# Routed experts' second product with weights at rest and tokens in motion, for four of eight experts

## The reference, cut to what matters

```python
def _L1_ffn_ref(x, Wr, W1, b1, W2, b2, sW1, sb1, sW2, sb2):
    logits = xf @ Wr.T
    topv, idx = jax.lax.top_k(logits, K)                 # K = 2
    gate_k = jax.nn.softmax(topv, axis=-1)
    ...
    h = jax.nn.relu(jnp.einsum('td,ehd->teh', xf, W1) + b1)
    y = jnp.einsum('teh,edh->ted', h, W2) + b2
    moe = jnp.einsum('te,ted->td', gates, y)
    sh = jax.nn.relu(xf @ sW1.T + sb1) @ sW2.T + sb2
    return moe + 0.1 * K * sh
```

## Time and profile before

| | value |
|---|---|
| timed runs, median (lowest to highest) | 2266.35 us (2262.14 to 2268.36) |
| profiled execution, its own time | 2264.78 us |
| span of its profile | 2263.6 us |
| TensorE busy in the span | 87% |
| VectorE busy | 60% |
| ScalarE busy | 40% |
| routed experts, from H(0) of e = 0 to the end of Y(7) of e = 7 | about 1522 to 2235 us of the span |

### The profile page before, as it was taken

How to read it: one execution, slowest core, us unless ns; L and a number is a source line. 1 busy time by engine, 2 the same in 40 slices (tenths; PEclk the granted TensorE clock), 3 DMA queues, 4 the chain that set the end, 5 groups by cost and what they waited for, 6 DMA issues and landing times.

```text
span 2263.6 us, 30780 instructions
## 1 busy us (share of the span) xinstructions
PE 1961.5 (87%) x12259; PEld 1831.3 (81%) x12260; DVE 1361.4 (60%) x2445; ACT 895.7 (40%) x1433; POOL 212.0 (9%) x177
## 2 busy tenths in 40 slices
PE   5787989878997975688758999999999999999984
PEld 5675779878887975587647989999999989888883
DVE  5878666442335466688865475446565665666675
ACT  2212212313231421366633322325555555555662
POOL 0000000003000000565720000000000000000001
PEclk9998998996999987799979899999999999999997
DMA  8100002100111100200021112224655566566775
GB/s 324 42 24 20 22 22 91 49 3 27 56 64 58 66 31 29 72 20 34 15 98 66 45 61 96 79 96 178 214 185 212 200 226 219 204 226 223 264 285 186
DMA packets 40346, 250.73 MB, mean 111 GB/s; under 512 B 5436, under 2 KB 6838, under 8 KB 18184
## 3 DMA queue, kind: packets, MB, share of 16 engines
q1 hardware_dynamic: 32024, 219.33, 27.2%
q10 hardware_dynamic: 5424, 16.52, 1.8%
q0 software_dynamic: 2752, 12.88, 1.7%
HBM read 225.80 MB, written 22.91 MB: 110 GB/s over the span
## 4 chain that ended last, share of the span: by engine, by line
PE 67%; DVE 17%; issue 9%; ACT 4%; DMA 3%; POOL 1%; DVEq 0%; POOLq 0%; SPq 0%; ACTq 0%
PE bank L280 18%; PE bank L282 17%; PE bank L281 17%; PE bank L2340 6%; DVE weight_lo L254 3%; PE bank L533 3%; PE bank L2341 3%; ACT weight_hi L244 2%; DMA weight_raw<-in_ffn_w 1%; PE bank L2344 1%; DVE mix_kv_lo L301 1%; DVE mix_kv L1531 1%; DMA token_rows<-expert_rows,slot_row 1%; DVE weight_lo L301 1%; DVE xT_lo L301 1%
## 5 line engine op out<-in xcount | busy, mean ns | idle before, releaser
L254 DVE TENSOR_TENSOR weight_lo<-weight_raw,weight_hi 128x2304 fp32r<-128x2304 f32 (+1 forms) x180 | 453.0, 2523 | 233.6 <-ACT weight_hi L244 233.4
L244 ACT ACTIVATE weight_hi<-weight_raw 128x2304 fp32r<-128x2304 f32 (+1 forms) x180 | 375.5, 2093 | 168.8 <-DMA weight_raw<-in_ffn_w 138.5
L280 PE MATMUL bank<-weight_hi,hidden_hi 128*128 128x384 f32 (+4 forms) x912 | 310.4, 340 | 12.5 <-DVE weight_lo L254 10.6
L282 PE MATMUL bank<-weight_hi,hidden_lo 128*128 128x384 f32 (+4 forms) x912 | 308.5, 338 | 0.0
L281 PE MATMUL bank<-weight_lo,hidden_hi 128*128 128x384 f32 (+4 forms) x912 | 308.1, 338 | 0.0
L280 PE MATMUL bank<-xT_hi,weight_hi 128*128 128x306 f32 (+1 forms) x576 | 185.0, 321 | 6.3 <-DVE mix_kv L1533 2.5
L281 PE MATMUL bank<-xT_lo,weight_hi 128*128 128x306 f32 (+1 forms) x576 | 179.6, 312 | 0.0
L282 PE MATMUL bank<-xT_hi,weight_lo 128*128 128x306 f32 (+1 forms) x576 | 179.1, 311 | 0.0
L280 PEld LDWEIGHTS bank<-weight_hi,hidden_hi 128*128 128x128 f32 (+4 forms) x912 | 159.0, 174 | 24.7 <-DVE weight_lo L254 12.6
L280 PE MATMUL bank<-weight_hi,xT_hi 128*128 128x384 f32 (+1 forms) x480 | 162.3, 338 | 10.0 <-DVE xT_lo L301 4.5
L533 PE MATMUL bank<-one_hot_dst,one_hot_src 125*128 125x313 f16 x800 | 130.0, 316 | 45.6 <-DVE one_hot_dst L511 42.4
(11 more groups left out here) (401 smaller groups left out, 4303.7 us busy)
## 6 DMA issues: line engine op xcount, KB each, us to landing
weight_raw<-in_ffn_w SPq DMA_DIRECT2D x136, 1152.0 KB, 5.2
weight_raw<-in_shared_w SPq DMA_DIRECT2D x16, 1152.0 KB, 5.2
expert_rows<-bias_row ACTq DMA_DIRECT2D x1, 12288.0 KB, 39.4
weight_raw<-in_mix_kv SPq DMA_DIRECT2D x8, 1152.0 KB, 6.8
weight_raw<-in_gat_w SPq DMA_DIRECT2D x8, 768.0 KB, 4.3
weight_raw<-in_mix_q SPq DMA_DIRECT2D x4, 1152.0 KB, 5.2
weight_raw<-in_mix_out SPq DMA_DIRECT2D x4, 1152.0 KB, 5.1
weight_raw<-in_gnn_w SPq DMA_DIRECT2D x4, 1152.0 KB, 5.1
```

The source lines that it names most:

```text
L244: act.activation(whi[:, r, 0:width[i]], raw[:, r, 0:width[i]], ACT.Copy).then_inc(*w_hi.one())
L254: dve.tensor_tensor(wlo[:, r, 0:width[i]], raw[:, r, 0:width[i]], whi[:, r, 0:width[i]].bitcast(F32), ALU.subtract).then_inc(*w_lo.one())
L280: pe.matmul(dst, a[0], b[0], start=first, stop=False)
L282: return pe.matmul(dst, a[1], b[0], start=False, stop=last)
```

## The change

For experts e = 2 to 5 (`ASIDE`; widths 208, 176, 160, 160) the second product is turned round. `w2` is at rest, 128 of its 768 output columns at a time, and the hidden units of all tokens move, upper and lower side by side. The sums come out transposed, one bank for each of six groups d of output columns, so they take six banks (2 to 7) and leave the ring two (0 and 1) for as long as these experts last. During the next expert's chunks 0 and 1 ScalarE copies the upper columns of each bank to `yT`, VectorE adds the lower columns (`y_out`). In its chunks 1 to 4 TensorE transposes `yT` back, one piece of three transposes a chunk behind Y, and ScalarE copies the piece to `yt`. The copy at the expert's end goes away for these four. For all experts the gathered tokens are turned one piece a chunk (chunks 1 to 4) in place of all in chunk 1. On ScalarE and VectorE the piece comes ahead of the chunk's two weight tiles.

```diff
+ASIDE = range(2, 6)
-        hT = tuple(part[:, :, :, 0:CAP] for part in hs)
+        hp = [part... "p (m a n) -> p m a n", m=3, a=2) for part in hs]
-        slot_bank, y_banks = psum[7], psum[4:8]
+        slot_bank, y_banks, yT_banks = psum[7], psum[4:8], psum[2:8]
+        Y_OUT = {(0, 0): (0, 1), (0, 1): (2, 3), (0, 2): (4,), (1, 0): (5,)}
+        def pieces(e, c):
+            return [c - 1] if e < E and 1 <= c <= 2 * len(tiles_of[e]) else []
...
+            def aside(bank, w, d, h, width, first, last):
+                both, one = bank[:, 0:2 * width].rearrange("p (a n) -> p a n", a=2), bank[:, 0:width]
+                hi, lo = at(w, ALL, ALL, slice(d * P, (d + 1) * P))
+                for k in range(3):
+                    if k < 2:
+                        pe.matmul(both, hi[:, k, :], h[:, k, :, 0:width], start=(first and k == 0), stop=False)
+                        pe.matmul(one, lo[:, k, :], h[:, k, 0, 0:width], start=False, stop=False)
+                    else:
+                        pe.matmul(one, lo[:, k, :], h[:, k, 0, 0:width], start=False, stop=False)
+                        end = pe.matmul(both, hi[:, k, :], h[:, k, :, 0:width], start=False, stop=last)
+                return end
+            def y_turn_tensor(e, j):
+                n, half = divmod(j, 2)
+                a0, rows = tiles_of[e][n]
+                pe.wait_ge(*y_sum.at(KD * (e - ASIDE[0] + 1)))
+                bank = ring.next(y_kept.at(turns_until[e] + j + 1))
+                for k in range(3):
+                    end = pe.transpose(bank[0:rows, k * P:(k + 1) * P], yT[:, 3 * half + k, a0:a0 + rows], ident[:, :])
+                end.then_inc(*y_turned.one())
             for e in range(E):
+                if e == ASIDE[0]:
+                    ring_parted = ring.until[2:4]
+                    ring.banks, ring.until, ring.k = psum[0:2], ring.until[0:2], ring.k % 2
+                if e == ASIDE[-1] + 1:
+                    summed = KD * (len(ASIDE) - 1)
+                    ring.banks, ring.until, ring.k = psum[0:4], ring.until + [y_sum.at(summed + 1), y_sum.at(summed + 2)], ring.k % 2
...
-                    if c == 1 and e + 1 < E:
-                        turn_tensor(e + 1)
+                    for j in pieces(e + 1, c):
+                        turn_tensor(e + 1, j)
...
+                        elif c == 1 and e - 1 in ASIDE:
+                            pe.wait_ge(*y_sum.at(KD * (e - ASIDE[0])))
...
+                        if e in ASIDE:
+                            for d in range(KD):
+                                end = aside(yT_banks[d], w, d, hp[g % 2], CAPS[e], first=(c == 1), last=(c == NCH))
...
+                    if e - 1 in ASIDE:
+                        for j in pieces(e - 1, c):
+                            y_turn_tensor(e - 1, j)
...
                         hidden_part(e, 3 * g)
+                        y_out(e, c, 0)
                         hidden_part(e, 3 * g + 1)
+                        y_out(e, c, 1)
                         hidden_upper(e, 3 * g)
                         hidden_part(e, 3 * g + 2)
+                        y_out(e, c, 2)
...
+                    for j in pieces(e + 1, c):
+                        turn_scalar(e + 1, j)
+                    if c < NCH:
                         weights_hi(place["ffn1_w1", e, c])
-                    if c == 1 and e + 1 < E:
-                        turn_scalar(e + 1)
+                    if e - 1 in ASIDE:
+                        for j in pieces(e - 1, c):
+                            y_turn_scalar(e - 1, j)
                     if c > 0:
                         weights_hi(place["ffn1_w2", e, c - 1])
+                if e in ASIDE:
+                    continue
                 act.wait_ge(*chunk_done.at(NCH * (e + 1)))
```

More of the change, by code:

```diff
@@ L48 @@
 CAP = MAIN * P
+ASIDE = range(2, 6)
+assert all(2 * CAPS[r] <= 512 for r in ASIDE)
 ROWS = [sum(CAPS[:r]) for r in range(E + 1)]
@@ L2292, in route_tensor, with turn_tensor @@
                     end.then_inc(*slot_hot_used.one())
-        def turn_tensor(e):
+        def turn_tensor(e, j):
             r = e % 2
+            n, c = divmod(j, 2)
+            rows = tiles_of[e][n][1]
             pe.wait_ge(*gathered[r].at(16 * sum(len(tiles_of[i]) for i in range(r, e + 1, 2))))
[L2297 to L2303, removed]
+            bank = ring.next(xe_lo.at(len(turn_banks) + 1))
+            turn_banks.append(bank)
+            for k in range(3):
+                end = pe.transpose(bank[:, k * P:k * P + rows], xg[0:rows, r, n, (3 * c + k) * P:(3 * c + k + 1) * P], ident[0:rows, 0:rows])
+            end.then_inc(*turned.one())
         def shared_tensor():
@@ L2319, in shared_tensor @@
                 if c == NCH:
-                    turn_tensor(0)
+                    for j in range(2 * len(tiles_of[0])):
+                        turn_tensor(0, j)
                 if c > 0:
@@ L2393, in route_scalar, with turn_scalar @@
                 upper(at(b2p, ALL, ALL), bias0[0:E, :]).then_inc(*b2_hi.one())
-        def turn_scalar(e):
+        def turn_scalar(e, j):
             r = e % 2
[L2397 to L2406, removed]
+            n, c = divmod(j, 2)
+            a0, rows = tiles_of[e][n]
+            i = turns_until[e] + j
+            if e < 2:
+                act.wait_ge(*sh_full.at(6 * NCH))
+            else:
+                act.wait_ge(*r_full.at(3 * NCH * (e - 1)))
+            act.wait_ge(*turned.at(i + 1))
+            act.activation(xe[r][:, 3 * c:3 * c + 3, 0, a0:a0 + rows],
+                           turn_banks[i][:, 0:3 * P].rearrange("p (k n) -> p k n", k=3)[:, :, 0:rows], ACT.Copy).then_inc(*xe_hi.one())
         def shared_scalar():
@@ L2435, in shared_scalar @@
                 if c == NCH:
-                    turn_scalar(0)
+                    for j in range(2 * len(tiles_of[0])):
+                        turn_scalar(0, j)
                 if c > 0:
@@ L2609, in shared_vector @@
                 if c == NCH:
-                    turn_vector(0)
+                    for j in range(2 * len(tiles_of[0])):
+                        turn_vector(0, j)
                 if c > 0:
@@ L2759, in vector @@
                         dve.wait_ge(*s_act.at(2 + 8 * c + 2 + 2 * (m + 1)))
[L2760 removed]
+                        lower(at(h_spilt, ALL, m, slice(0, P)), ht[:, 0, 0:P]).then_inc(*s_dve.one())
             sync()
```

83 lines of the change are left out of this document (60 added, 23 removed).

## The result

The changed kernel takes 2331.64 us in the median of four runs (2325.33 to 2342.42). The ratio to the kernel before is 1.0299, with a 95% interval of 1.0253 to 1.0345, so it is about 67 us slower than the kernel before, whose four runs beside it have a median of 2264.68 us. The forecast was 2301 us with a range of 2274 to 2336. The direction and the mechanism were right; the size was that of rival (a), 2331 us.

What follows compares the result with a forecast made beforehand. TensorE's work bounds the kernel before; a loop of waits on two banks bounds the changed one. Stretches +14.0, crossings +12.7 and pieces -1 give +26 us, the clock +10: 2264.8 + 26 + 10 = 2301 us, range 2274 to 2336.

Steps and rivals of the forecast that it cites:

- rival (a): TensorE's clock falls at every new idle time, costing 40 us in place of 10: 2331 us; chance 0.12.
- What bounds: At e = 2 to 5 TensorE's own work sets the time, being busy for nearly all of some 70 us.
- Second product: At e = 2 to 5 a new Y costs as an H of its width; 43 us less TensorE work.
- Rival (d): New Ys are not as fast as Hs; even at 6.28 us the time would not move; counted in the forecast's 0.74.
- The ring of two banks: In each chunk m2 waits for m0's sum; period 12.19 us at 208, 12.02 at 176, 11.94 at 160.
- Turned tokens by pieces: Pieces ahead of w2(c)'s parts cost nothing at e = 2 to 5; e = 0 and 1 save 1 us.
- Turning the sums back: In chunks 1 to 4 of e = 3 to 5 ScalarE waits for the piece; 6.5 us more.
- Crossings: From H(7) to the next expert's H(1), sums behind lower parts add 12.7 us; 5 to 6 unchanged.
- TensorE's clock: Half clock behind two thirds of seven long and one in ten of 18 short new idle times: +10 us.
- (b): TensorE stays the bound and the change does what its column count says: 2227 us; chance 0.09.
- (c): The loop of waits is there but the parts cancel: 2266 us within 0.3%; chance 0.05.

Runs made afterwards that it cites:

- the kernel with fillers: The changed kernel with twelve zero-matrix matmuls ahead of TensorE's wait for m0's bank, in chunks 2 to 7 of e = 3 to 5: 2310.64 us.
- the copy-late kernel: The changed kernel with ScalarE's copy of the turned-back piece moved behind the upper part of w1(c+2): 2310.09 us, ratio 1.0184.

## Why the prediction was right, and where its size was off

**What bounds.** Right. At full clock TensorE's own work set these stretches, and the chain of the earlier trace rows lay 10.28 us behind H's end without cost. (Of the idle time in the earlier trace rows I had misread one end: it is 1.1 to 1.3 us, not 1.1 to 1.5. Nothing hangs on it.) Turning by pieces took away the idle time of the earlier trace rows and left TensorE busy for every moment of the stretches of e = 2 to 5.

**Second product.** Right where it could be seen: at full clock a new Y takes 4.67 us at 160 (between 2006.84 and 2011.50 in the kernel with fillers), as long as an H. Rival (d) had no part in it.

**The ring of two banks.** Right, and now shown three ways: 62 us of waits for VectorE's sum, 44 us by narrowing the ring with nothing else changed, and 71 us back by an order that brings the sums out of the weights' shadow. The period at 208 was forecast at 12.19 us and measured at 12.2 to 12.7; with fillers the four last chunks without a piece at 160 took 11.9 to 13.0 against 11.94.

**Turned tokens by pieces.** Costs nothing, as forecast, and gives more than the 1 us I took off: e = 0 and 1 were 2.2 us shorter and e = 6 by 3.0, for which I had put down nothing. As a kernel of its own it gives about 10 us, since there the idle time of the earlier trace rows goes in every expert, and with it the half-clock stretches; in the changed kernel the stretches of e = 2 to 5 are set by the loop and don't show it.

**Turning the sums back.** The mechanism was right, ScalarE waiting for the piece ahead of w1(c+2). The price, 0.48 to 0.72 us a chunk, held roughly with fillers (12.6 to 13.2 us for the four chunks of e = 4 with a piece, 12.42 forecast). The 1.7 us that I wrote for e = 5 have no working beside them; at 0.48 us a chunk they would be 1.9. The price did not hold at half clock. I wrote that of a slow piece only m2 lies on the loop and that Y, m0 and m1 have idle time to spare. In chunks 1 to 4 that is wrong: a slow Y makes the piece late, this holds ScalarE, and the loop runs through Y after all. The twelve chunks with a piece at e = 3 to 5 took 12.7 to 16.0 us.

**Crossings.** +12.7 us forecast, 23.7 measured. The two-bank ring alone makes them 5.4 to 5.5 us longer with none of `y_out`; the halved clock behind waits of 2.6 to 2.9 us, which I had put under another heading, is in that. For 5 to 6 I had said that the shorter Ys make up for the wait for banks 2 and 3. They don't: m2 waited 2.99 us for `y_out`'s add there, and its crossing is 2.9 us longer.

**TensorE's clock.** This is the step that failed in size. I took one in ten of the 18 short idle times because the clock had stayed up after 2.06 us and fallen after 2.48. The new ones were 1.2 to 2.8 us, twelve of them 2.2 to 2.4, and behind 14 of the 18 the clock fell to half, two of 1.70 and 1.85 us among them. It stayed up behind 1.24, 1.74, 2.17 and 2.30 us, each of which began 5.5 to 6.5 us after the end of a half-clock stretch. So the length of an idle time alone does not tell what follows it. The trace of before had this in it already. The earlier trace rows show 3.4 us behind the idle time of 2.06 us at full clock; but 4.2 us after it TensorE was idle once more, and then the clock was at half. At e = 6 it was at half behind 1.96 us:

```profile
1000.76 0.91 PE L1793 MATMUL bank<-identity,gat_edge 128*128 128x128 f32 x5 [1.12 <-POOL gat_edge L1750]
2106.54 0.55 PE L2302 MATMUL bank<-identity,token_rows 128*128 128x128 f32 x3 [1.96 <-DVE hidden_tmp L2630]
```

```profile
1001.30:1004.60 3.30, 3.30 (x13) 3.30 (x11) 3.30 (x6) 2.90 (x8) 3.30 (x3) 0.50 0.00 0
2107.20:2110.50 3.30, 3.30 (x12) 3.30 (x11) 1.46 (x5) 3.13 (x5) 0.00 (x0) 0.50 0.56 223
```

The stretches of e = 3 to 5 ran at 0.85 to 0.88, so 12% to 15% short of full speed, which is 24% to 30% of their time at half. Of my +10 us, 2.9 were for these 18 idle times; the fillers show about 24 us in the same three stretches. Rival (a), with 0.12, had named this. The clock at full speed, at half and back again in nearly every chunk is what the section "A second HAM failure mode: psum-queue depth-cycling" of the Trainium skill's page "TensorE: Matmul & The Clock Gate" describes for a bf16 kernel that cycles through PSUM banks, and with 14 falls behind 18 idle times this trace agrees. The 40 us of (a) came out near the total in part by chance, since it too left out the way through ScalarE and had the crossings at +12.7 us.

**Rivals (b) and (c)** fall with the time.

## What to carry to other kernels

When a change takes banks of PSUM away from a ring, find in the trace when each bank is really given back, not when its matmuls end. With strict order on the engines that empty it, the read can stand behind long work for a later stage, and four banks had hidden that. Where a second engine's order is what makes the wait, move the short operation ahead before widening anything, and price a TensorE idle time of about 2 us that comes back every chunk as one that may also cost the clock. In the changed kernel 14 of 18 idle times of 1.2 to 2.8 us did. Two rows of a trace, one on each side, are no threshold: look at every idle time of that length that the trace has, and at what comes after it.

## What I had not expected of the hardware

Adding 216 matmuls of zeros made the kernel 21 us faster. Idle times of mostly 2.2 to 2.4 us in each chunk of 12 to 16 us left TensorE at half clock for 24% to 30% of the time. In the same three stretches with filler work ahead of them, idle times of 0.2 to 1.7 us were never followed by half clock. In the copy-late kernel the chunks with a piece have idle times such as 0.74 and 0.57 us, 1.9 us apart; the clock stayed up in nine of these twelve chunks and fell in the other three.
